# Routing weights loaded during the last attention, rows 0 to 2 normalised there, and one of two roundings at the row ends moved to ScalarE

## The reference

```python
x = x + 0.5 * ffn(layernorm(x))
x = x + attn(layernorm(x))
x = x + 0.5 * ffn(layernorm(x))

def ffn(x):                       # 16 heads of 32, 8 experts, top 2
    logits = x.reshape(b, -1) @ switch_w.T + switch_b     # one choice for a whole row of 512 x 512
    gate, top_idx = top_k(softmax(logits), 2)
    h = gelu(per_head(x) @ w1[top_idx] + b1[top_idx])
    o = sum over the two of gate * (h @ w2[top_idx] + b2[top_idx])
    return (x + o) @ w3.T + b3

def attn(x):                      # linear recurrence in chunks of 64
    q, k, v, a, g = split(x @ w_in.T, 5)
    q = q * rsqrt(mean(q * q) + eps);  k = tanh(k);  a = clip(sigmoid(a + 2), 0.6, 0.9995)
    memory = scan over tokens with decay a of k * v
    return (sigmoid(g) * (q * memory) + (1 - sigmoid(g)) * v) @ w_out.T
```

## Time and profile before

| | |
|---|---|
| median of 3 runs | 589.83 us (588.72 to 590.0) |
| the profiled execution | 588.68 us, its span 587.0 us |
| TensorE products | 507.7 us busy, 87% of the span, 3349 instructions |
| TensorE loads of the stationary operand | 361.7 us, 62% |
| VectorE | 427.4 us, 73% |
| ScalarE | 219.8 us, 37% |
| GpSimd | 138.3 us, 24% |

### The profile page before, as it was taken

How to read it: one execution, slowest core, us unless ns; L and a number is a source line. 1 busy time by engine, 2 the same in 40 slices (tenths; PEclk the granted TensorE clock), 3 DMA queues, 4 the chain that set the end, 5 groups by cost and what they waited for, 6 DMA issues and landing times.

```text
span 587.0 us, 9023 instructions
## 1 busy us (share of the span) xinstructions
PE 507.7 (87%) x3349; PEld 361.7 (62%) x3372; DVE 427.4 (73%) x796; ACT 219.8 (37%) x367; POOL 138.3 (24%) x141
## 2 busy tenths in 40 slices
PE   0375899999899999999999999999999447799997
PEld 0363676666586666658666666766667344577776
DVE  3769887997974777796477798735886777997752
ACT  0126644423615233261433344233330027666540
POOL 5140012454001224401322410122330101311220
PEclk9985999999999999999999999999999877999999
DMA  9987004000002000010200001030117940013012
GB/s 277 377 341 315 1 0 163 0 1 1 36 19 88 3 0 2 1 37 19 89 0 0 0 0 54 0 125 1 55 54 321 380 162 2 8 46 127 36 55 89
DMA packets 16612, 48.21 MB, mean 82 GB/s; under 512 B 1600, under 2 KB 1856, under 8 KB 15296
## 3 DMA queue, kind: packets, MB, share of 16 engines
q1 hardware_dynamic: 15760, 47.19, 21.4%
q10 hardware_dynamic: 816, 0.54, 0.5%
HBM read 39.33 MB, written 8.39 MB: 81 GB/s over the span
## 4 chain that ended last, share of the span: by engine, by line
PE 57%; DVE 14%; issue 14%; POOL 6%; SPq 4%; DMA 3%; ACT 2%; DVEq 0%; POOLq 0%
PE bank L386 9%; PE bank L388 8%; PE bank L387 8%; PE bank L684 7%; PE bank L689 7%; PE bank L685 7%; POOL rs L1056 4%; SPq L412 4%; DMA route_w<-in_switch_w 3%; DVE h_lo L1252 2%; DVE h_hi L1251 2%; PE bank L537 1%; POOL rs_wide L1061 1%; PE bank L519 1%; PE bank L595 1%
## 5 line engine op out<-in xcount | busy, mean ns | idle before, releaser
L684 PE MATMUL bank<-xh,win_hi 128*128 128x512 f32 x300 | 133.7, 446 | 0.0
L685 PE MATMUL bank<-xl,win_hi 128*128 128x512 f32 x300 | 118.0, 393 | 0.0
L689 PE MATMUL bank<-xbf,win_lo 128*128 128x512 bf16 x289 | 80.1, 381 | 1.5
L1056 POOL TENSOR_TENSOR rs<-ms,neg_half 128x16 f32<-128x16 f32 x16 | 49.8, 3113 | 130.3 <-ACT ms L898 130.3
L684 PEld LDWEIGHTS bank<-xh,win_hi 128*128 128x128 f32 x300 | 56.5, 188 | 21.0 <-issue 3.2
L685 PEld LDWEIGHTS bank<-xl,win_hi 128*128 128x128 f32 x300 | 56.5, 188 | 11.1
L1043 POOL TENSOR_TENSOR xa<-xa,b_half 128x512 f32<-128x512 f32 x28 | 40.6, 1462 | 64.0 <-DVE z_lo L1270 31.6
L386 PE MATMUL bank<-w_hi,z_hi 128*128 128x512 f32 x128 | 51.6, 403 | 0.0
L388 PE MATMUL bank<-w_hi,z_lo 128*128 128x512 f32 x128 | 50.0, 391 | 0.0
L387 PE MATMUL bank<-w_lo,z_hi 128*128 128x512 f32 x128 | 49.9, 390 | 0.0
L835 ACT ACTIVATE hf<-bank,w_sel 128x512 f32<-128x512 f32 x64 | 41.9, 689 | 17.6 <-DVE h_lo L1252 8.1
(11 more groups left out here) (186 smaller groups left out, 1036.8 us busy)
## 6 DMA issues: line engine op xcount, KB each, us to landing
route_w<-in_switch_w SPq DMA_DIRECT2D x4, 2048.0 KB, 14.4
route_w<-in_switch_w SPq DMA_DIRECT2D x16, 512.0 KB, 16.2
raw<-in_w_in SPq DMA_DIRECT2D x4, 1280.0 KB, 10.3
xa<-in_x SPq DMA_DIRECT2D x4, 1024.0 KB, 6.7
out<-x SPq DMA_DIRECT2D x16, 256.0 KB, 2.0
x_dram<-x1p SPq DMA_DIRECT2D x12, 256.0 KB, 2.0
xa<-x_dram SPq DMA_DIRECT2D x3, 1024.0 KB, 5.7
x_chunk<-in_x SPq DMA_DIRECT2D x2, 1024.0 KB, 23.6
```

The costliest lines, as they stand in the source:

```text
L684: pe.matmul(bank[:], win_hi[:, c, r, k, :], xh[:, k, :], start=(k == 0), stop=False)
L685: pe.matmul(bank[:], win_hi[:, c, r, k, :], xl[:, k, :], start=False, stop=False)
L689: mm = pe.matmul(bank[:], win_lo[:, c, r, k, :], xbf[:, k, :], start=False, stop=(k == KC - 1))
L1056: pool.tensor_tensor(rs[:], ms[:], neg_half[:], ALU.pow).then_inc(s_rs, 1)
```

## The change

It has five pieces.

1. **Weights in pieces.** `late_weights(c)` loads, as soon as group c's projections of the last row are made, those columns of `route_w` that lie on `win_hi[:, c]` and `win_lo[:, c]`; the last four of 64 slices, on `gt` and `starts`, follow behind `yt`. All nine loads count on one semaphore, `s_swl`, for which TensorE waits once.
2. **Rows 0 to 2 in the last attention.** Events 4 to 7 are now tiles 0 to 3 of rows 0 to 2, events 8 to 11 those of row 3. Statistics of event 4 + c run within group c (`gap`), in front of the multiplication of `qt`. Tiles 0 and 1 are normalised by VectorE behind groups 0 and 1, tiles 2 and 3 by ScalarE (`x * rstd + shift`, with `shift = -mean * rstd` from GpSimd) behind group 2 and behind the last `y_out`, into buffers of their own (`xn_h`, `xn_z`), which lie on memory that is dead by then.
3. **Behind the attention.** Output tiles go in a new order; VectorE's four events of row 3 are interleaved, so that each normalise comes behind the next tile's sum and statistics. ScalarE normalises row 0 into `xn_0` (`first_row`), from a load of x2's row 0 that is issued in front of the stores.
4. **Behind the routing.** One `xt_split`, then `select(0, B, 0)`, then the other three. ScalarE loads gelu's table right after the exponential.
5. **Row ends** of rows 1 to 3: `second_hi` on ScalarE rounds expert 2 of each chunk; VectorE only waits for it and subtracts.

```diff
+        def normed(n):
+            _, t, lo, hi = EVENTS[n]
+            if n < FEW + 2:
+                return n + 1
+            assert n >= LAST
+            return n - 1
...
+        LATE_PIECES = []
+        for c in range(KC):
+            LATE_PIECES.append((ROLES * (c + 1), [(10 * c, 10 * c + 10), (40 + 5 * c, 45 + 5 * c)]))
```

SyncE:

```diff
             chunk_load(x2_dram, 0, B - 1)
             chunk_load(x2_dram, 1, B - 1)
-            sp.wait_ge(s_rn, event(1, 0, False))
+            late_weights(0)
+            sp.wait_ge(s_rn, normed(FEW))
             chunk_load(x2_dram, 2, B - 1)
-            sp.wait_ge(s_rn, event(1, 1, False))
+            late_weights(1)
+            sp.wait_ge(s_rn, normed(FEW + 1))
             chunk_load(x2_dram, 3, B - 1)
-            sp.wait_ge(s_in, IN_JOBS * B)
-            for t in range(NT - 1):
-                weight_load(t)
+            late_weights(2)
+            late_weights(3)
             sp.wait_ge(s_y, KC * B)
-            weight_load(NT - 1)
+            late_piece(60, 64)
+            sp.wait_ge(s_rna, 1)
+            sp.dma_start(xa[:], row_of(x2_dram, 0)).then_inc(s_xa, 16)
+            sp.wait_ge(s_rna, 2)
+            sp.dma_start(x1p[:], row_of(x2_dram, 2)).then_inc(s_xa2, 16)
             for t in range(NT):
                 store_x2(B - 1, t, x1, job_last(f"A{t}"))
-            sp.wait_ge(s_rn, event(1, 2, False))
-            sp.dma_start(xa[:], row_of(x2_dram, 0)).then_inc(s_xa, 16)
             sp.wait_ge(s_rm, 2 * NT)
             sp.dma_start(xa1[:], row_of(x2_dram, 1)).then_inc(s_xa1, 16)
-            sp.dma_start(x1p[:], row_of(x2_dram, 2)).then_inc(s_xa2, 16)
```

TensorE:

```diff
-            for chunks in (range(KC - 1), range(KC - 1, KC)):
-                for t in range(NT):
+            most_k, last_k = range(KC - 1), range(KC - 1, KC)
+            for t, chunks in ((0, most_k), (1, most_k), (2, most_k), (0, last_k), (1, last_k),
+                              (3, most_k), (2, last_k), (3, last_k)):
```

ScalarE:

```diff
+            def second_hi(f, c):
+                src, hi, _ = hid_set(f, c)
+                if c == 0:
+                    act.wait_ge(s_sel[1], f + 1)
+                else:
+                    act.wait_ge(s_ob, job_ffn(f, f"O{c - 1}") + 1)
+                act.wait_ge(s_gelu, H_JOBS * f + TOPK * c + TOPK)
+                act.activation(hi[:, 1, :], src[:, 1, :], ACT.Copy).then_inc(s_hh, 1)
```

```diff
+            def route_norm(t):
+                act.wait_ge(s_rs2, t + 1)
+                for b in range(B - 1):
+                    ins = act.activation(dst, src, ACT.Identity, scale=rstd[:, b, t:t + 1], bias=shift[:, b, t:t + 1])
+                ins.then_inc(s_rna, 1)
...
-            attention(B - 1)
+            attention(B - 1, lambda c: route_norm(c) if c == 2 else None)
             y_out(B - 1, KC - 1)
+            route_norm(NT - 1)
+            first_row()
...
             route_exp(1)
+            load_table(ACT.Gelu)
```

GpSimd:

```diff
+                if FEW <= n < LAST:
+                    pool.wait_ge(s_rp, n + 1)
+                    pool.tensor_tensor(shift[:, lo:hi, t], neg_mu[:, lo:hi, t], rstd[:, lo:hi, t],
+                                       ALU.mult).then_inc(s_rs2, 1)
```

VectorE:

```diff
-                    own.do(ve.tensor_copy(hi[:, k, :], src[:, k, :]))
+                    if k == 1 and not (isinstance(f, int) and f == 0):
+                        ve.wait_ge(s_hh, KC * (f - 1) + c + 1)
+                    else:
+                        own.do(ve.tensor_copy(hi[:, k, :], src[:, k, :]))
...
                 pref_done = own.mark(ve.tensor_tensor_scan(pref[:], decay[:], starts[:], 0.0, ALU.mult, ALU.max))
+                gap(c)
                 ve.wait_ge(s_rst, KC * b + c + 1)
...
-            attention(B - 1, early)
+            attention(B - 1, lambda c: route_norm(FEW + c) if c < 2 else None,
+                      lambda c: route_var(FEW + c, route_stats(FEW + c)))
             for t in range(NT):
                 out_add(t, job_last(f"A{t}"), last_bank[t], x1, x1)
-                if t < 2:
-                    ve.wait_ge(s_obf, job_last(f"A{t}") + 1)
-                    route_event(NT + 2 + t)
-            ve.wait_ge(s_obf, late_base)
-            for n in range(NT + 4, len(EVENTS)):
-                route_event(n)
-            ve.wait_ge(s_rm, 2 * NT - 1)
-            normalise(B, 0)
+                ve.wait_ge(s_obf, job_last(f"A{t}") + 1)
+                m = route_stats(LAST + t)
+                if t >= 1:
+                    route_norm(LAST + t - 1)
+                route_var(LAST + t, m)
+            route_norm(LAST + NT - 1)
             choose(1)
-            for c in range(KC):
+            xt_split(B, 0)
+            select(0, B, 0)
+            for c in range(1, KC):
                 xt_split(B, c)
-            select(0, B, 0)
```

## The result

The changed kernel takes **578.58 us** (median of 4 runs, 577.89 to 579.71) against 589.41 for the kernel before in the same comparison (4 runs, 588.72 to 590.0): a ratio of 0.9829, 95% interval 0.981 to 0.9848. It is faster by 10.8 us; 17.2 were forecast, to 572.6. Its profiled execution took 579.71 us with a span of 578.0 (before: 588.68 and 587.0).

What follows compares the result with a forecast made beforehand. TensorE is busiest, but VectorE's chain sets the end before expert choice and delays row ends. Savings 3.7 + 12.0 + 1.5 = 17.2 us give 571.5 profiled, 572.6 as median; range 567.5 to 579.

Steps and rivals of the forecast that it cites:

- Row ends: Three row ends: ScalarE takes one of VectorE's two roundings, so TensorE waits less; 3.7 us, bounds nothing to 4.1.
- (a): Last attention: routing weights load in pieces as projection columns die; what remains after 441 takes 6 us, landed by 450.
- (b): Last attention's groups: statistics of rows 0 to 2 between scan and scale multiplication cost 2.6 us, delaying y in group 3.
- (c): Last attention: earlier rs_wide (0.9, TensorE's wait about 0.45) and faster decay clipping give back; y_low of chunk 3 moves +1.3.
- (d): Between groups 2 and 3: ScalarE's normalise of chunk 2 could delay TensorE's q_sums by nothing to 0.7 us; nothing taken.
- (e): Output tiles: TensorE starts at 440.9 instead of 441.83, then waits for y_low, a new gap of 1.6 us.
- (f): VectorE after output tile 0: 2.3 us per tile instead of 2.95, last normalise done at 459.6.
- (g): Second routing on TensorE: four blocks of 2.0 us at full clock, just behind VectorE, the last ending at 462.1.
- (h): Second routing: pauses from late instructions cost 1.8 us, some 1.2 at the first place and 0.3 at each later two.
- The starved rival: Second routing: each of three instruction portions takes 5.8 us, routing ends at 473.0, total 581.6; chance 13%.
- Part 3: After expert choice starts: earlier select, gelu table load and row 0 normalise bring gelu and h_lo forward; 1.5 us (1.2 to 1.8).
- Slower by the clock: From the routing on: TensorE's clock falls and stays low, stretching later work by at most 82 us, up to 655; chance 3%.

Runs made afterwards that it cites:

- undone kernel: Changed kernel with second_hi taken out, so VectorE rounds both experts again at the row ends: 581.77 us, ratio 0.9894.
- stores-behind kernel: Changed kernel with the load of x2's row 2 and the last row's four x2 stores issued behind the routing: 576.17 us, ratio 0.9798.
- the held clock: On the stores-behind kernel, 18 and 14 unread products fill TensorE's waits before and after hidden(0) of the last row: 574.73 us, ratio 0.9765.
- the kernel with the statistics one tile later: Stores behind, clock-holding products, and tile 3 statistics of rows 0 to 2 moved behind row 3's tile 1 normalise, against changed kernel: 572.66 us, ratio 0.9723.

## Why the prediction was wrong

**Row ends (3.7, bounds nothing to 4.1): nearly right.** The trace gives 0.77, 1.04 and 1.01, 2.8 in all; the medians of the undone kernel give 3.2. The mechanism is the one forecast: ScalarE rounds in 0.63 beside VectorE, and one row end gains 1.04 where 1.25 was forecast. TensorE still waits 0.35 for the h_lo at 259.45. The size was taken from one row end, and 3.7 was near its upper bound.

**(a) Weights: right.** Nothing waits for them; the first routing block runs its 128 products in 1.99.

**(b), (c) y_low: +1.3 forecast, +1.8 measured** (446.66 + 1.81 = 448.47 against 446.65). The statistics took 2.38 from start to start (437.41 to 439.79) and not 2.6, and decay 0.41 in each group as said. The Trainium skill, "SBUF — State Buffer", section "SBUF: two separate sides", with its shared port of VectorE and GpSimd, agrees with the 0.41, where it had been 1.26 with GpSimd at work. Two things were overlooked. GpSimd's rs_wide now runs beside y_lo, which took 0.99 (434.69) in place of 0.69, so 0.3 of the 0.85 is lost again; before the change it was

```profile
436.53 0.69 DVE L1353 TENSOR_TENSOR y_lo<-yt,y_hi 128x512 fp32r<-128x512 f32 x1 [1.06 <-ACT y_hi L877]
```

And the other is (d).

**(d) nothing: wrong by 0.4.** ScalarE began the three normalisations of tile 2 at 425.96, they took 2.23, and the square of q came right behind them; TensorE's q_sums waited for it:

```profile
428.71 0.42 PE L645 MATMUL bank<-q_sq,heads 128*32 128x128 f32 x8 [0.38 <-ACT q_sq L945]
```

TensorE's two waits for rs_wide did go as said, some 0.45 each, but this one gave back 0.38. So group 3 began where it had begun before, y_low had none of the 0.45, and the output tiles start at 439.53 + 1.81 = 441.34, 0.5 earlier and not 0.9. The terms, 2.38 - 0.86 + 0.31 - 0.03, give the 1.8.

**(e) gap of 1.6: right**, 1.45. **(f) 2.3 us per tile, the last normalise done at 459.6: right in its end.** A tile takes 2.05 (450.20 to 452.25 from sum to sum), which makes good the 0.5 that y_low came later: 457.74 + 1.81 = 459.55. That the sum is right is luck, two misses that cancel.

**(g) and (h): here the prediction fails.** Its term (h), 1.8 us for late instructions, was mis-sized. From the place in block 1 to the end of the last pause the forecast has 8.4 us (464.0 - 453.8 - 1.8), 2.8 for each of three portions; they took 5.95, 3.44 and 3.61, 13.0 in all, 4.6 more. Block 1 started 0.65 later than forecast. With 0.1 in the rest these are the 5.4 of the 12.0 that are missing. In pauses it is 5.86 against 1.8.
The cause had been named rightly, and two things in its size were wrong. First, the rings were taken as full until about 455; the load of x2's row 2 and the four stores of the last row's x2, which the change leaves just there, filled them to 458 (379 GB/s in 456 to 458). Moving them shortened the first portion by 3.1 and the way to T by 2.65. Second, the two later places were put at 0.3 each by the last block of the kernel before, which had no pause. That block had started 5.2 us after the pause in the one ahead of it had ended, since the block ahead ran at the half clock (3.41) and TensorE then waited for VectorE, and its portion had arrived in that time. Faster VectorE took this cover away: with empty rings a portion takes 2.9 to 3.9 us and TensorE 2.0, so each one costs 0.9 to 1.9.
The half clock behind the pause of 3.95 was a sign of error that the prediction had named (the clock falls before T), but it cost next to nothing up to T. Block 2 took 1.2 longer by it, and the next pause was 0.29, where it is 1.62 with the full clock in the stores-behind kernel; in the kernel with the row ends undone two blocks ran at the half, and T minus anchor was the same. A slow TensorE waits less for portions that come no faster.
The starved rival was the other end of the same sum, each portion at 5.8, and T at 473.0; T is at 467.56 + 1.81 = 469.4, between forecast (464.0) and rival. One of three portions took what the rival said.
The Trainium skill, "Runtime: NRT & Kernel Launch", section "Instruction fetch mechanics", calls the crossing of a block mostly hidden; here the first crossing, in block 1, shows no pause in any run, but at the three others TensorE lost up to 4.0 us, and nothing only where it had waited for VectorE or run at the half clock just before; the trace decides.

**Part 3 (1.5): its events were right, its gain wasn't.** Gelu's first result comes at T + 10.26 (10.3 forecast), and O0 at T + 13.43, 1.5 earlier against T than before. But 0.9 of it is given back. The granted clock, 0.50 from 476 on (TensorE had worked 1.5 of the 6 us before), rose only when layer 1 of chunk 2 was being done at 484.84, 3.9 us after O0; before it was back 1.4 us after O0. Products of 0.63 in place of 0.40 delay the chain, and behind the third expert output TensorE waits 2.17 for z_lo, where it waited 1.39; from O0 to that transpose it is 11.28 against 10.35 before:

```profile
480.99 0.76 PE L406 MATMUL bank<-h_hi,w_hi 128*128 128x512 f32 x1
...
484.84 0.45 PE L581 MATMUL bank<-xt_lo,w_hi 64*128 64x512 f32 x2
...
492.27 0.66 PE L559 MATMUL bank<-ident_r,xnw 128*128 128x128 f32 x4 [2.17 <-DVE z_lo L1366]
```

and in the kernel before:

```profile
501.25 0.66 PE L519 MATMUL bank<-ident_r,xnw 128*128 128x128 f32 x4 [1.39 <-DVE z_lo L1270]
```

The forecast had named it as up to 2 us more if the clock did not fall in this gap; the held clock measured 1.95.

**The rivals.** Row ends that give nothing: refuted by the undone kernel. More gained with no starvation: refuted by the pauses. A y delayed by 3.3: it was 1.8. Slower by the clock: it fell in two places and came back each time, at no cost up to T and at 0.9 us behind it. That rival's worst case also rests on a slip: 111.0 us lie behind T (587.0 - 475.98) and not 123, so it was 74 more and not 82.

**What stays open.** Why the clock came back 2.7 us later in the first routing of this execution is not known; that of the kernel with the statistics one tile later shows the same (0.50 to about 41, choose(0) at 43.89), and all others had choose(0) at 42.7 to 43.0. Nor is it known why a portion takes 2.9 in one place and 3.9 in another with empty rings. Whether fewer instructions (a loop over the products) would do away with the pauses wasn't tried.

## What to carry to other kernels

An engine that executes many short instructions in a row also needs them to arrive: count the pairs of load and product, look for pauses with no releaser at equal distances, and price each at the time of a portion less the time of its execution. Such pauses are hidden for as long as the engine waits for another one or runs slowly, so a change that makes the other engine faster uncovers them. Transfers that nobody waits for still belong elsewhere than into such a stretch, and where a matrix engine must wait near the end of a chain, products that nobody reads can hold its clock.

## What the runs showed of the hardware

- 128 products with their 128 loads arrive in 2.9 to 3.9 us with empty DMA rings and in 5.5 to 7.2 us with full ones (250 to 410 GB/s); TensorE executes them in 2.0 us at the full clock, in 3.4 at the half.
- Such a portion is one packet of 16 KB on a queue of its own. With empty rings it started 0.5 to 1.8 us after TensorE took up the portion before, with full ones 3.3 to 4.8 us after; TensorE went on 2.2 to 2.8 us behind its start in either case.
- Twenty small float32 products are 40 loads and 40 products in the trace, and they moved the pauses by 40 pairs.
- After a pause of 3.95 us TensorE's clock was at its lower level, 1.2 GHz (0.50 in 458 to 460), until about 461; after a wait of 2.40 us for VectorE a block also took 3.39. With pauses of 0.86, 1.62 and 1.89 in the same stretch it stayed at 1.00.
- 32 products that nobody reads (18 and 14 of 128 x 512, 4.35 and 3.47 us) keep the clock at 2.4 GHz over the choice of experts and save 1.4 us by the medians, 1.95 in the trace.
- A VectorE operation beside GpSimd's rs_wide: the clipping of 128 x 512 took 1.26 us in place of 0.41, the subtraction y_lo 0.99 in place of 0.69.
